# Attention layers of a graph network: two of five mask products move from POOL to DVE, fused with the limit of the exponential

## The reference

```python
def _gat_conv(x, src, dst, W, a_src, a_dst, b, n_nodes):
    h = x @ W
    alpha_s = h @ a_src
    alpha_d = h @ a_dst
    e = alpha_s[src] + alpha_d[dst]
    e = jnp.where(e > 0, e, NEG_SLOPE * e)          # NEG_SLOPE = 0.2
    m = jax.ops.segment_max(e, dst, num_segments=n_nodes)
    m = jnp.where(jnp.isfinite(m), m, 0.0)
    ex = jnp.exp(e - m[dst])
    s = jax.ops.segment_sum(ex, dst, num_segments=n_nodes)
    alpha = ex / (s[dst] + 1e-16)
    out = jax.ops.segment_sum(alpha[:, None] * h[src], dst, num_segments=n_nodes)
    return out + b

h = relu(_gat_conv(x, ..., W1, a1s, a1d, b1)); h = relu(_gat_conv(h, ..., W2, ...)); return _gat_conv(h, ..., W3, ...)
```

## Time and profile before

| | |
|---|---|
| time, median of 3 runs | 2073.58 us |
| the profiled execution, its own time | 2075.87 us |
| its span | 2074.0 us |
| the attention steps | from about 1319 to 1919 us of the span |
| busy in these 600 us: PE, DVE, ACT, POOL | 538.07, 467.06, 489.35, 508.44 us |
| the same over the whole span | 1681.0, 1490.4, 1158.5, 1115.0 us |

### The profile page before, as it was taken

One profiled execution on the slowest core, in us unless ns is written; L12 is line 12 of the kernel. 1 busy time (PEld: TensorE's weight loads), 2 busy tenths in 40 slices (PEclk: granted clock), 3 DMA queues, 4 the chain that ended last, 5 costly groups with the idle time before them and its releaser, 6 DMA issues. The chain is left out here.

```text
span 2074.0 us, 36733 instructions
## 1 busy us (share of the span) xinstructions
PE 1681.0 (81%) x9771; PEld 854.7 (41%) x9772; DVE 1490.4 (72%) x3987; ACT 1158.5 (56%) x2276; POOL 1115.0 (54%) x983
## 2 busy tenths in 40 slices
PE   1777777684799999999899895799979997999675
PEld 0222222352344444444444444545344534443444
DVE  5999999435577777777777674678857896788554
ACT  5777777312344444444444442489858985898211
POOL 1000000001777777777777772399959994999200
PEclk9999999897899999999999996799989998999877
DMA  7000000101111111111111114000000000000000
GB/s 183 0 0 0 0 0 0 77 1 54 31 41 34 39 35 34 39 35 39 34 34 39 34 29 121 5 1 1 1 1 1 1 1 1 1 1 8 9 1 16
DMA packets 29632, 50.72 MB, mean 24 GB/s; under 512 B 12820, under 2 KB 13826, under 8 KB 29054
## 3 DMA queue, kind: packets, MB, share of 16 engines
q1 hardware_dynamic: 11890, 31.59, 5.1%
q0 software_dynamic: 17664, 18.12, 5.1%
HBM read 36.58 MB, written 7.39 MB: 21 GB/s over the span
## 5 line engine op out<-in xcount | busy, mean ns | idle before, releaser
L809 POOL DMA_INDIRECT adj<-h_table,l_idx x544 | 570.0, 1048 | 166.4 <-issue 157.8
L1541 POOL TENSOR_TENSOR gat_ring<-gat_ring,adj 125x750 f32<-125x750 f32 (+2 forms) x375 | 507.7, 1378 | 91.4 <-ACT gat_ring L1595 85.8
L999 DVE TENSOR_SCALAR adj<-adj,node_key 125x1024 f16<-125x1024 f16 x825 | 380.2, 503 | 203.9 <-PE psum L944 180.9
L944 PE MATMUL psum<-adj,x_sb 125*128 125x512 f16 x1650 | 403.7, 389 | 1.3 <-DVE adj L999 1.3
L1448 DVE SCALAR_TENSOR_TENSOR gat_ring<-x_sb,gat_node,psum 125x750 f32<-125x750 f32 (+2 forms) x375 | 315.8, 859 | 89.3 <-PE psum L1669 48.8
L387 PE MATMUL psum<-col_hot,src_hot 128*128 128x500 bf16 x808 | 205.6, 376 | 114.9 <-DVE src_hot L316 93.5
L872 ACT ACTIVATE l_z<-psum 128x320 f32<-128x320 f32 x204 | 89.2, 437 | 343.4 <-PE psum L923 343.3
L1666 PE MATMUL psum<-gat_ring,gat_hx 125*65 125x500 f32 (+1 forms) x500 | 250.1, 585 | 17.9 <-POOL gat_ring L1541 16.2
L721 POOL MEMSET l_aggT<- 64x3146 f32 x1 | 2.7, 2713 | 478.1 <-POOLq L1730 478.1
L313 DVE TENSOR_SCALAR col_hot<-iota_h,c_tab 128x500 bf16<-128x500 f16 x808 | 227.4, 345 | 25.1 <-PE psum L387 21.1
L1592 ACT ACTIVATE gat_ring<-gat_ring,gat_node 125x750 f32<-125x750 f32 (+2 forms) x267 | 217.7, 815 | 41.9 <-DVE gat_ring L1448 38.8
(11 more groups left out here) (241 smaller groups left out, 2080.5 us busy)
## 6 DMA issues: line engine op xcount, KB each, us to landing
adj<-h_table,l_idx POOLq DMA_INDIRECT x544, 2.6
adj<-key_table SPq DMA_DIRECT2D x33, 250.0 KB
adj<-adj SPq DMA_DIRECT2D x3, 1662.5 KB
adj_saved<-adj SPq DMA_DIRECT2D x1, 3840.3 KB
adj<-adj_saved SPq DMA_DIRECT2D x5, 688.2 KB
x_sb<-in_x SPq DMA_DIRECT2D x1, 781.2 KB
x_saved<-x_sb SPq DMA_DIRECT2D x1, 781.2 KB
out<-x_sb SPq DMA_DIRECT2D x5, 156.2 KB
```

The source lines that it names most:

```text
L809: pool.indirect_dma_start(out=to[:, t, :], out_offset=None, in_=table[:, :], in_offset=bass.IndirectOffsetOnAxis(ap=index[:, t:t + 1], axi ...
L944: last = pe.matmul(psum[:, PAIR[half] + t, :], h_parts[:, k, :], select[0:P, k % SELECTS, t * GE:(t + 1) * GE], start=(k == 0), stop=(k == ...
L999: v.tensor_scalar(select[0:P, k % SELECTS, :], keys, node_key[:, k:k + 1], None, ALU.is_equal).then_inc(s_sel, 1)
L1541: pool.tensor_tensor(slot, slot, adj[:, k, cols(c)], ALU.mult).then_inc(s["weight_ready"], 1)
```

## The change

A step n with `n % 5` in (1, 3) is now masked by DVE (`masked_by_dve`), in every chunk; since 125 is a multiple of 5, these are k = 1, 3, 6, 8, ..., ten of the 25 steps. In them DVE computes only the exponent at first (L1452), ACT one exponential with the bias `a` (L1605), and then DVE one operation, `mask(n)` (L1463): slot = min(slot, 1) * adj. This rests on exp(min(y, 0)) = min(exp(y), 1). POOL leaves these steps out. In the other fifteen steps ACT does its two operations and POOL the product, as before. DVE's limit L1453 no longer exists. PE waits for one of two semaphores, by the step.

`mask(n)` stands in DVE's program behind the exponent of step n+2 (`MASK_LAG = 2`), and waits there for ACT.

```diff
@@ -1251,6 +1251,7 @@
     LAYERS, STEPS = 3, GC * NT
     ROW1 = 6
     PROJECT_AT, ABSORB_AT, SUMMED_AT, NODE_AT = 6, 11, 17, 20
+    MASK_LAG = 2
     WXC = D + 3
 
     row_parts = (slice(0, EVEN), slice(EVEN, P))
@@ -1262,7 +1263,7 @@
     names = ("agg_transposed", "x_added", "vecs_in", "x_kept", "ln_chain", "ln_centred", "ln_squared", "ln_var", "ln_std", "ln_chunk",
              "self_loops", "w_chain", "w_columns", "w_rows", "constants", "transposed", "transpose_copied", "first_projected",
              "first_read", "shift_chain", "extremes", "extremes_all", "starts", "levels_ready", "levels_summed", "node_rows", "row1_in_psum",
-             "row2_in_psum", "row2_copied", "exponent_raw", "exponent_ready", "exponent_bounded", "exp_ready", "weight_ready", "product_done",
+             "row2_in_psum", "row2_copied", "exponent_ready", "exponent_bounded", "exp_ready", "weight_ready", "dve_weight_ready", "product_done",
              "sums_copied", "projected", "absorbed", "degrees_read", "degrees_final", "x_last", "x_done")
     s = {n: sem("gat_" + n) for n in names}
     s_tail = {t: sem(f"gat_tail_back{t}") for t in range(TAIL, NT)}
@@ -1276,11 +1277,14 @@
     def width(c):
         return GCHUNK[c] * P
 
-    def bounded_by_dve(c, k):
-        return k % 2 == 1 if c == GC - 1 else k % 4 == 3
-
-    def bounded_to(g, k):
-        return sum(bounded_by_dve(i // NT % GC, i % NT) for i in range(g * NT + k + 1))
+    def masked_by_dve(n):
+        return n % 5 in (1, 3)
+
+    def dve_masks_to(n):
+        return sum(masked_by_dve(i) for i in range(n + 1))
+
+    def pool_masks_to(n):
+        return n + 1 - dve_masks_to(n)
 
     def level_sums_of(g, rows=P):
         return psum[0:rows, 4 + g % 2, 0:GCHUNK[g % GC] * LEVELS].rearrange("p (t j) -> p t j", j=LEVELS)
@@ -1447,11 +1451,17 @@
                 slot = ring[:, n % RING, 0:width(c)]
                 op = v.scalar_tensor_tensor(by_tile(slot), by_tile(rrow[:, 0:width(c)]), k_s[:, k:k + 1],
                                             in_psum(ROW1, c), ALU.add, ALU.max)
-                if bounded_by_dve(c, k):
-                    op.then_inc(s["exponent_raw"], 1)
-                    dve.wait_ge(s["exponent_raw"], bounded_to(g, k))
-                    op = v.tensor_scalar(slot, slot, asd[:, g // GC % 2, 0, k:k + 1], 0.0, ALU.add, ALU.min)
                 op.then_inc(s["exponent_ready"], 1)
+
+            def mask(n):
+                if not masked_by_dve(n):
+                    return
+                g, k = divmod(n, NT)
+                c = g % GC
+                slot = ring[:, n % RING, 0:width(c)]
+                dve.wait_ge(s["exp_ready"], n + 1)
+                v.scalar_tensor_tensor(slot, slot, 1.0, adj[:, k, cols(c)], ALU.min, ALU.mult)\
+                    .then_inc(s["dve_weight_ready"], 1)
 
             def absorb(g, i):
                 layer, c = divmod(g, GC)
@@ -1499,11 +1509,15 @@
                     g = first + c
                     for k in range(NT):
                         exponent(g, k)
+                        if c > 0 or k >= MASK_LAG:
+                            mask(g * NT + k - MASK_LAG)
                         if c > 0 and ABSORB_AT <= k < ABSORB_AT + ops:
                             absorb(g - 1, k - ABSORB_AT)
                         if c + 1 < GC:
                             for i in {NODE_AT - 1: (0,), NODE_AT: (1, 2), NODE_AT + 1: (3, 4, 5)}.get(k, ()):
                                 node_step(g + 1, i)
+                for n in range((first + GC) * NT - MASK_LAG, (first + GC) * NT):
+                    mask(n)
                 for i in range(ops):
                     absorb(first + GC - 1, i)
             dve.wait_ge(s["absorbed"], absorbed_to(LAYERS * GC - 1))
@@ -1537,6 +1551,8 @@
                     for k in range(NT):
                         n = (layer * GC + c) * NT + k
                         slot = ring[:, n % RING, 0:width(c)]
+                        if masked_by_dve(n):
+                            continue
                         pool.wait_ge(s["exp_ready"], n + 1)
                         pool.tensor_tensor(slot, slot, adj[:, k, cols(c)], ALU.mult).then_inc(s["weight_ready"], 1)
 
@@ -1585,8 +1601,8 @@
                         if c + 1 < GC and k == NT - 1:
                             row2_out(g + 1)
                         act.wait_ge(s["exponent_ready"], n + 1)
-                        if bounded_by_dve(c, k):
-                            act.activation(slot, slot, ACT.Exp).then_inc(s["exp_ready"], 1)
+                        if masked_by_dve(n):
+                            act.activation(slot, slot, ACT.Exp, bias=asd[:, layer % 2, 0, k:k + 1]).then_inc(s["exp_ready"], 1)
                         else:
                             bounded += 1
                             act.activation(slot, slot, ACT.Relu, scale=-1.0, bias=neg_a_s[:, k:k + 1])\
@@ -1660,7 +1676,10 @@
                 n = g * NT + k
                 if k == 0:
                     pe.wait_ge(s["row2_copied"], g + 1)
-                pe.wait_ge(s["weight_ready"], n + 1)
+                if masked_by_dve(n):
+                    pe.wait_ge(s["dve_weight_ready"], dve_masks_to(n))
+                else:
+                    pe.wait_ge(s["weight_ready"], pool_masks_to(n))
                 sums, hx = pair(sums_of(g), D + 1), feats[layer % 2]
                 near = min(GCHUNK[c], 4)
                 last = pe.matmul(sums[:, 0:near, 0:P], hx[:, k, :], by_tile(ring[:, n % RING, 0:near * P]),
```

## The result

The changed kernel takes 2057.84 us (median of 4 runs, 2056.04 to 2060.13) against 2073.12 us beside it: ratio 0.9928, 95% interval 0.9911 to 0.9945, 15.3 us less. Forecast were 2055 us, 18.6 less than the 2073.58 shown at first. Measured once more beside other kernels (e10), the ratio was 0.9916 (0.9901 to 0.9930).

The account below looks back on a forecast made before the run. PE and POOL were taken as near the limit at 750 columns, POOL alone at 500. Chunk gains of 0, 1.0, 1.0, 2.5 and 1.8 us make 6.3 a layer, 18.9 in three: 2055 us, own range 2046 to 2065.

Parts of the forecast that it names:

- PE's floor of the second chunk: Second chunk, 750 columns: PE's products, level sums, row spreads and projection need at least 41.3 us.
- the floor of 40.8: Third chunk, 750 columns: PE's own work needs at least 40.8 us.
- Rival 2: Whole kernel: locks align fully, only PE's and ACT's floors are left; 31 us gained, 2043 us, chance 0.20.
- the cycle of five steps: Steady 750-column steps, paced by PE: each mask falls between POOL's operations, with about 1 us to spare.
- w: A DVE mask's wait for POOL: taken as 0.2 us in steady steps, 0.4 overall in crowded ones around chunk changes.
- The estimate of the mask's price from L1401 and L1448: DVE's mask L1463, priced from similar operations: 916 ns at 750 columns, 649 ns at 500.
- Rival 1: Whole kernel: masks meet POOL at full length and DVE becomes the bound; 29 us slower, 2103 us, chance 0.16.
- the fourth chunk: Fourth chunk, 750 columns: from 42.51 us, with PE's floor at 38.5, a gain of 2.5 us a layer.
- the one for the change of chunks: Chunk changes: late masks cost at most 6 us over twelve, set against L1429 and followers finding POOL idle more often.
- the mask of step 23: Chunk change, mask behind the next chunk's first exponent: hidden to w = 1.0, costing at most 0.5 us at w = 1.5.
- My own sign for rival 1: L1463's mean above 1.42 us, or PE waiting for L1463 by name over 5 us a layer, would show it.
- ACT's floor: 500-column chunk: ACT becomes the bound at 26.2 us for 25 steps; a gain of 1.8 us a layer was taken.

Follow-up runs that it names:

- e10: The changed kernel unaltered, measured again beside other kernels: 2057.52 us, ratio 0.9916 to the kernel before.
- e8: Changed kernel with the new mask rule in the 500-column chunk alone, the other chunks as before: ratio 0.9978 to the kernel before.
- e5: Changed kernel with the first node step (L1429) moved behind the exponent and mask that follow it: ratio 0.9846 to the kernel before.
- e9: Changed kernel with later first node step and masks at n % 5 in (0, 2): 2032.23 us, ratio 0.9803 to the kernel before.
- e4: Changed kernel with the mask's second tensor row1 in PSUM instead of adj in SBUF, except step 23: 2059.14 us, ratio 0.9925 to before.
- e3: Changed kernel with DVE's mask L1463 left out, so part of the work is missing: 2038.47 us, ratio 0.9822 to the kernel before.
- e6: Changed kernel with masked steps n % 5 in (0, 2) instead of (1, 3): ratio 0.9833 to the kernel before.
- e7: Changed kernel with the exponential of masked steps (L1605) lacking its bias: ratio 0.9937 to the kernel before.
- e11: The kernel before, without the change, with only the first node step moved later: 2079.28 us, ratio 1.0026 to the kernel before.
- e1: Changed kernel with the mask one step behind its exponent instead of two: 2081.03 us, ratio 1.0034 to the kernel before.
- e2: Changed kernel with the mask three steps behind its exponent instead of two: 2133.90 us, ratio 1.0286 to the kernel before.

## Why the prediction came out as it did

**Right in the whole, partly by luck.** POOL and PE were both near the limit, and the time fell inside the forecast's own range. e8 shows that the 500-column chunk's gain comes from the change within it. But the change relieves POOL, gives ACT one operation less in some steps and takes L1453 from DVE, and no run does these one by one, so the share of each is argued. And the total is better than its parts: over three layers the measured gains differ from the forecast by 1.6 us more in the second chunk, 2.0 and 5.4 less in the third and fourth, 2.5 more in the fifth and 1.3 less elsewhere.

**Wrong: PE's floor of the second chunk.** I put it at 41.3 us, and e5 took 39.63 and e9 38.65 in the first layer. A window from one copy of row2 to the next holds 25 products, but four of them belong to the chunk before: in after the copy is at 1344.95 and four products of 375 columns still follow, 0.81 to 0.91 us apart, which I priced at 1.47. Four times some 0.6 us less is 2.5, and 41.3 - 2.5 = 38.8. That after took just 41.30 us there is a coincidence: PE is busy 38.44 of them and waits the other 2.9. In the same way the window of the fifth chunk holds four products of 750 columns, which my sum for it did not have. For the third chunk the floor of 40.8 holds (40.93 in e9, PE busy 40.82 of them). Rival 2's 2043 us, meant as the floor of all, is 11 us above e9.

**Right: the cycle of five steps.** w was near 0 in steady steps: 0.982 us against 0.93 at 750 columns. Between the changes of chunks PE ran at 1.46 to 1.47 us a step with six level sums and at 1.41 with four. The estimate of the mask's price from L1401 and L1448, 0.916 us, is within 2% of 0.934 (the median). Rival 1, DVE bound by the locks, fell: e4 takes nearly all the locks away and gains nothing that can be measured. One reading was off without harm: 1.507 us is the median of L1541 over all three widths; at 750 columns its mean is 1.624, so 15 steps are 24.4 us and not 22.6 (measured 24.85 and 24.63 in the third and fourth chunk).

**Mis-sized: the fourth chunk.** I took 2.5 us a layer and 0.7 came. The floor itself can be reached: 38.5 us predicted, 38.6 in e3's first layer (115.1 over three). The term that failed is the one for the change of chunks. I had followed the mask of step 23, which was hidden as I said (product 23 comes 1.26 to 1.47 us after product 22), and set the rest against each other. The mask of step 18 stood two places behind an operation that waits for PE, and I never named it, although the diff puts the mask behind the exponent of step 20 and the first node step ahead of that exponent, and the old trace had the wait of that node step (L1425 there, L1429 in after):

```profile
DVE x_sb L1425 <- PE psum L1637: 22.0, 14, 3.5
```

6.9 of these 22.0 us are the starts of two layers; the twelve changes of chunks have 1.0 to 1.4 us each, on DVE, where it hurt less. The same stall keeps the third chunk at 1.0 of 3.0 us, and stands in the second (1.0 us of PE's waiting). It is not the whole of the fourth chunk's: e5, e6 and e9 still take 120.3 to 120.7 us there, and what holds these 5 us over e3 is open. My own sign for rival 1, PE waiting over 5 us a layer for L1463, came true for the loads of weights (28.9 us, 9.6 a layer) and nearly for the products (14.3 us, 4.8 a layer), for a cause that is not rival 1: a late mask, not a busy DVE. A wait by name does not say which.

**Mis-sized the other way: the 500-column chunk.** 7.9 us came, 5.4 were taken. The window of 32 us was foreseen, but ACT's floor as its one bound was wrong (e7), and ACT is busy 27.71 of 31.87 us in it, not over nine tenths. In its last steps ACT and DVE are both full, as e7 showed; without masks the window is 30.6 us (e3). PE still waits there for POOL, 10.9 us of weight load in the first layer, for masks 4.2. No run relieves ACT and DVE together, so the bound is not settled by experiment.

**Missed: the bias.** L1605 takes 0.908 us where I used 0.829. The earlier trace rows had it: L1592, with a bias from gat_node, at 0.911 us stands beside L1595, without one, at 0.829. It cost nothing that can be measured (e7).

**What else fell in.** The attention layers began 1.8 us earlier in the profile of after, at 1316.31 instead of 1318.12 us, which is not the change's: e10 had 1314.79 and e11 1315.01. Without it the profiles differ by 14.9 us.

## What to carry to other kernels

When an operation is moved to an engine that works in order, list what stands ahead of it there, and among these look for each one that waits for a third engine: the moved operation inherits that wait, and so does whoever needs it. In this kernel the place in the order was worth more than the change itself, with the same instructions: 25 us (e9) against 15. And when a window is priced by steps, count whose steps they are: a cut at one engine's event holds other steps on the next engine. A handover can be late in both directions: one step earlier it waits for its producer (e1), one step later its consumer waits (e2).

## What was not expected of the hardware

Of DVE and POOL, whichever starts first holds up the other until it is done. The longest L1557 of after took 2.361 us where the shortest took 1.508, which is 0.85 us more, and a mask is 0.93 long. Shifting the mask by one step turned the bill round: 1.283 us for the mask and 1.573 for POOL at lag 1, 0.982 and 1.640 at lag 2. A bias per partition on ACT's exponential costs 0.09 us (0.908 against 0.815 us at 750 columns, 0.698 against 0.606 at 500). The Trainium skill says so too: "ScalarE: Activation LUTs", section "What ACT_TABLE_LOAD costs", gives about 93 ns for each such operand.
